# Where GpSimd's value copies stand among its weight splits, and when ScalarE copies chunk 52, in a graph-attention layer with a quantised FFN

## The reference

```
y  = layernorm(x)
q, k, v    = y @ wq.T + bq, y @ wk.T + bk, y @ wv.T + bv
q2, k2, v2 = q @ wiq.T + biq, k @ wik.T + bik, v @ wiv.T + biv   # 16 heads of 64
mask[src, dst] = softplus(edge_type_weights)[type - 1], else -inf   # last edge wins; diagonal filled
attn = softmax(q2 @ k2.T / 8 + mask);  x = x + (attn @ v2) @ wo.T + bo
z  = fake_quant(layernorm(x));  h = fake_quant(silu(z @ wg.T) * (z @ wu.T))   # int8 levels
x  = x + h @ wd.T
```

## Time and profile before

| | |
|---|---|
| median of 3 runs | 406.78 us (405.72 to 407.1) |
| profiled execution | 405.72 us |
| its span | 404.0 us |
| busy PE | 354.1 us, 88% of the span |
| busy DVE | 281.0 us, 70% |
| busy POOL | 203.1 us, 50% |
| busy ACT | 176.4 us, 44% |
| chain that ended last | PE 59%, POOL 15%, ACT 8%, issue 7%, DVE 6%, DMA 5% |
| mean granted clock of TensorE | 0.961 |

### The profile page before, as it was taken

How to read it: one execution, slowest core, us unless ns; L and a number is a source line. 1 busy time by engine, 2 the same in 40 slices (tenths; PEclk the granted TensorE clock), 3 DMA queues, 4 the chain that set the end, 5 groups by cost and what they waited for, 6 DMA issues and landing times.

```text
span 404.0 us, 6371 instructions
## 1 busy us (share of the span) xinstructions
PE 354.1 (88%) x2016; PEld 303.1 (75%) x2017; DVE 281.0 (70%) x642; ACT 176.4 (44%) x339; POOL 203.1 (50%) x270
## 2 busy tenths in 40 slices
PE   0869998697899999999998999999998769995972
PEld 0769986475677777899997899999998558882631
DVE  4999799986577876353325597798788654496377
ACT  2532325253632113143434586686677455225520
POOL 2698978445252533578882526635647664000003
PEclk9999999899899999999999899999999979997888
DMA  8454784555122122134341113113204231000004
GB/s 294 142 196 144 265 291 159 182 196 170 53 65 92 52 76 80 54 104 134 125 158 54 49 56 105 52 54 104 69 38 157 88 111 33 30 0 2 0 0 157
DMA packets 14212, 42.32 MB, mean 105 GB/s; under 512 B 1908, under 2 KB 3180, under 8 KB 14188
## 3 DMA queue, kind: packets, MB, share of 16 engines
q1 hardware_dynamic: 13254, 40.80, 30.2%
q10 hardware_dynamic: 934, 1.22, 0.8%
HBM read 40.41 MB, written 1.61 MB: 104 GB/s over the span
## 4 chain that ended last, share of the span: by engine, by line
PE 59%; POOL 15%; ACT 8%; issue 7%; DVE 6%; DMA 5%; SPq 0%; ACTq 0%; POOLq 0%; DVEq 0%
PE PS L620 39%; POOL ring L358 13%; PE PS L695 6%; DMA stage<-in_weights 3%; PE PS L735 3%; PE PS L747 3%; ACT scratch L510 3%; PE PS L723 3%; PE PS L884 2%; ACT PT L446 1%; POOL X L371 1%; ACT ring L436 1%; POOL QT L381 1%; DMA V<-in_w_down 1%; PE PS L844 1%
## 5 line engine op out<-in xcount | busy, mean ns | idle before, releaser
L358 POOL TENSOR_TENSOR ring<-stage,ring 128x256 fp32r<-128x256 f32 x208 | 163.1, 816 | 110.8 <-ACT ring L436 110.8
L620 PE MATMUL PS<-XT,ring 128*128 128x384 f32 x576 | 116.8, 348 | 4.3 <-issue 4.1
L620 PEld LDWEIGHTS PS<-XT,ring 128*128 128x128 f32 x576 | 100.2, 188 | 8.8 <-issue 5.3
L436 ACT ACTIVATE ring<-stage 128x1024 fp32r<-128x1024 f32 x52 | 54.3, 1058 | 14.1 <-DMA stage<-in_weights 14.0
L620 PE MATMUL PS<-ring,AT 128*128 128x512 f32 x144 | 38.0, 421 | 0.7 <-ACT V L478 0.7
L620 PE MATMUL PS<-QT,ring 128*128 128x384 f32 x192 | 36.2, 343 | 0.0
L620 PE MATMUL PS<-AT,ring 128*128 128x384 f32 x192 | 35.2, 338 | 0.0
L695 PE MATMUL PS<-scratch 128*128 128x384 bf16 x156 | 34.4, 330 | 0.0
L620 PEld LDWEIGHTS PS<-AT,ring 128*128 128x128 f32 x192 | 33.1, 188 | 1.5 <-issue 1.2
L510 ACT ACTIVATE scratch<-scratch,smx 128x384 f32<-128x384 f32 x48 | 28.9, 604 | 11.8 <-DVE smx L1107 11.8
L620 PEld LDWEIGHTS PS<-QT,ring 128*128 128x128 f32 x192 | 33.7, 191 | 0.3 <-issue 0.2
(11 more groups left out here) (176 smaller groups left out, 520.2 us busy)
## 6 DMA issues: line engine op xcount, KB each, us to landing
stage<-in_weights SPq DMA_DIRECT2D x56, 512.0 KB, 3.3
scratch<-key_rows SPq DMA_DIRECT2D x8, 448.0 KB, 4.1
V<-in_w_gate_up SPq DMA_DIRECT2D x5, 512.0 KB, 4.5
out<-X SPq DMA_DIRECT2D x6, 256.0 KB, 2.1
V<-in_w_down SPq DMA_DIRECT2D x6, 176.0 KB, 4.7
X<-in_x SPq DMA_DIRECT2D x2, 512.0 KB, 5.5
X<-in_x ACTq DMA_DIRECT2D x1, 512.0 KB, 5.1
guT<-in_bias_o ACTq DMA_DIRECT2D x1, 512.0 KB, 7.6
```

Source lines behind the costliest of these rows:

```text
L358: ins = pool.tensor_tensor(ring[1][:, slot, piece], stage[:, slot % STAGE, piece], ring[0][:, slot, piece].bitcast(F32), ALU.subtract)
L436: act.activation(ring[0][:, slot, :], stage[:, slot % STAGE, :], ACT.Copy).then_inc(w_high, 1)
L620: ins = pe.matmul(outs, lhs[a], rhs[b], start=start and n == 0, stop=stop and n == 2, skip_group_check=True)
```

## The change

In GpSimd's list `pair_v(1)` to `pair_v(4)` stand behind the low parts of chunks 40, 42, 44 and 46, `pair_v(5)` behind that of chunk 48, and `pair_v(6)` behind that of chunk 50: each comes one or two chunks later in the list than before, and what it does is the same. In ScalarE's list the high part of chunk 52 stands behind the exponentials of pair 7 and no longer ahead of `o_take(6, 0)`.

```diff
             pair_v(0)
-            for c in range(CPAIR + 4, 39):
+            for c in range(CPAIR + 4, 48):
                 low(c, c % RING)
-            for u in range(5):
-                pair_v(u + 1)
-                for c in (39 + 2 * u, 40 + 2 * u):
-                    low(c, c % RING)
+                if c % 2 == 0 and c >= 40:
+                    pair_v((c - 38) // 2)
+            low(48, 0)
+            pair_v(5)
             low(49, 1)
+            low(50, 2)
             pair_v(6)
-            low(50, 2)
             low(51, 3)
             spare_low(52)
             pair_v(7)
@@
             probs_high(6, 1)
             pair_high(50)
             pair_high(51)
-            spare_high(52)
             o_take(6, 0)
             exps(7, 0)
             exps(7, 1)
+            spare_high(52)
             o_take(6, 1)
             spare_high(53)
```

## The result

| | before | after |
|---|---|---|
| median | 406.94 us (4 runs) | 448.24 us (4 runs, 446.66 to 451.69) |
| profiled execution | 405.72 us | 452.39 us |
| its span | 404.0 us | 450.7 us |
| mean granted clock | 0.961 | 0.907 |

The ratio is 1.1017, with a 95% interval of 1.0934 to 1.1102: the change makes the kernel about 41 us slower. 444.5 us was forecast, 38.8 us above the profiled execution of before.

A forecast was written before the change was run, and what follows sets the result against it. TensorE was taken to bound the loop over head pairs, other engines having slack. Loop stalls of 24.7, the attention's end 4.5 and the clock 9.6 gave 38.8 us on 405.72 us: 444.5 us, range 434 to 454.

The forecast's parts named there:

- Step 1: Loop over head pairs: weighs 1 to 5 each wait about 4.9 us for GpSimd's pair_v, 24.7 us in all.
- Step 2: End of the attention, from weigh(5, 0): product with chunk 53 starts 4.5 us later, with a sixth idle stretch of 3.4 us.
- Step 3: TensorE behind the six new idle stretches: the clock falls to half, 1.6 us lost each, 9.6 us in all.
- rival (b): TensorE's new gaps: stalls come, each followed by two low-clock stretches or one much longer; 454.1 us, chance 0.17.
- Rival (a): TensorE's new gaps: the stalls come, but the clock holds through them; 434.9 us, chance 0.12.
- Rival (c): Loop: GpSimd, freed from waiting for VA, starts low parts earlier and pair_v comes in time; not slower, 402.6 us, chance 0.03.

The follow-up runs named there:

- e4: Kernel before, with pair_v(u + 1) in the loop moved between the two chunks' low parts, not behind both; 417.96 us, ratio 1.0249.
- e3: Kernel before, with only the second half of pair_v(u + 1) in the loop moved behind the two chunks; 405.8 us, ratio 0.9987.
- e2: Kernel before, with only ScalarE's high part of chunk 52 moved behind the exponentials of pair 7; 409.05 us, ratio 1.0041.
- e5: Changed kernel, with TensorE running idle matmuls in its waits before weigh(1, 0) to weigh(6, 0); 436.01 us, ratio 1.069 to the kernel before.
- e6: Kernel before, with only pair_v(6) moved behind the low part of chunk 50; 413.35 us, ratio 1.013.
- e7: Kernel before, with pair_v(6) behind chunk 50 and chunk 52's high part behind pair 7's exponentials, loop unchanged; 413.1 us, ratio 1.0202.
- e1: Kernel before, with only pair_v(1) to pair_v(5) in the loop moved behind the two chunks; 437.27 us, ratio 1.0713.

## Why the prediction was right, and where it was off

**Step 1, the loop's stalls, right.** Forecast were five waits of 4.9 us and a period of 19.32 us without the clock. The trace has 4.7 us before each weigh and weigh(1, 0) 19.22 us behind weigh(0, 0), 4.85 more than before; the kernel with its gaps filled has periods of 19.4 us. e4 scales the wait with the length of the queue, and e3 shows that only the half which the next weigh needs counts.

**Step 2, the end, right in its mechanism.** weigh(6, 0) was to start 16.55 us behind weigh(5, 0) plus the clock's part: 357.02 - 338.34 = 18.68, and the clock's part behind that gap is 2.2 us. From weigh(5, 0) to the product of chunk 53 it is 9.6 us more: 4.5 as forecast and 5.1 of clock behind two gaps, where 3.2 were forecast. The kernel with its gaps filled has 33.98 us for that way, against 33.85 forecast. From weigh(6, 0) to the product of chunk 53 it is 5.4 us more, the 2.5 of step 2 and 2.9 of clock. One statement of the step was wrong, though the sum does not rest on it: the wait of 3.60 us before weigh(6, 1) was not taken away. ScalarE's take is early now, but VectorE's part of the result stands behind the last mask tiles and ends at 367.60 us, and weigh(6, 1) starts at 367.70 after 2.93 us of idle time. The waits for chunks 52 and 53, 2.88 and 1.49 us, came on top, and the move of chunk 52 by itself costs (e2).

**Step 3, the clock, a term too small.** 1.6 us were charged behind each gap. From weigh(k, 0) to weigh(k, 1) it took 7.18 us before; after, 9.38, 8.84, 8.74, 10.10 and 9.38: losses of 2.2, 1.7, 1.6, 2.9 and 2.2 us. Behind the sixth gap the scores of pair 7 end 7.75 us behind the weigh's start instead of 4.80, 2.9 us lost. That is 13.5 us and not 9.6. The price was taken from single stretches of 3.40 us at low clock, and it fits the two gaps that had one such stretch, the second and the third (1.7 and 1.6 us). At the other four the clock was low for 6.8 to 6.9 us, twice as long. So what rival (b) describes, two low stretches to a gap, is what happened at four of six. Its 454.1 us is too dear all the same, since at the first and fifth gap 2.1 us of the low clock fell into idle time, where it costs nothing (2.2 us lost); where nearly all of it fell into work it cost 2.9 us, near the 3.2 that (b) charges. That the forecast lies nearer than (b) is so in part by luck. What decides between one stretch and two no run shows. Rival (a) is refuted by the stretches of the trace; e5 shows what holding the clock would have been worth, 3%.

In sum: 42.2 us in the stretch that the change touches against 38.8 forecast. The clock took 3.9 us more than its term and the stalls of the loop 0.4 us less (24.3). The median moved by 41.3 us.

**Rival (c) falls** by the changed kernel's own trace and by e3: freeing GpSimd from VA starts the chunks no earlier. The low parts at 246.43 us start 12.59 us behind weigh(0, 0), and those at 242.22 in the earlier trace rows start 12.59 us behind it too (229.63).

## What to carry to other kernels

In a hand-written list the price of an instruction's place is the time of what stands ahead of it since that was last released, against when its consumer needs it; an engine half idle can still be late, and a wait which another wait outlasts is worth nothing. Before putting a step off, look up its first consumer: here the second half of the same helper is needed 7 us later than the first, and that was enough. Where the moved step makes TensorE idle, charge the clock as well, as a range and not as one price; it made up a third of this loss.

## What the runs showed of the hardware that was not expected

- Whether the clock fell behind an idle time was not settled by its length: behind 2.0 us it fell at two of five gaps (the profiled execution of e4), behind 3.20 us it fell in e6 and held in e7, and behind 4.7 us it fell at all ten (the changed kernel and e1), at 1.5 to 2.9 us each.
- Executions of one kernel spread by some 2% (before: 401.96 to 410.64 us in one series). In the profiles the granted clock of the first weight chunks (30 to 98 us) is 0.90 to 1.00 for the same instructions, and weigh(0, 0) starts anywhere from 226.8 to 234.1 us. Single profiles are best compared from a mark behind that.
- Idle matmuls in the six waits (27 in each, 19 in the last) were worth 12 to 13 us: the waits for GpSimd became no shorter, but the work behind them ran at 2.4 GHz.
